# A sparse feed-forward with its pairs taken in three TensorE stages, deeper rings, and targets read from the row itself

## What is computed

```python
topk_idx, topk_weight = _gate(x, gate_w, e_bias)      # 4 of 16 experts per token
g = jnp.einsum('th,eih->eti', x, gate_proj)           # h = 256, i = 128
u = jnp.einsum('th,eih->eti', x, up_proj)
inter = jax.nn.silu(g) * u
expert_out = jnp.einsum('eti,ehi->eth', inter, down_proj)
sel = expert_out[topk_idx, jnp.arange(T)[:, None]]
y = jnp.einsum('tkh,tk->th', sel, topk_weight)
shared_out = jax.nn.silu(hidden_states @ shared_gate_w.T) * (hidden_states @ shared_up_w.T) @ shared_down_w.T
return y + shared_out
```

## Time and profile before

| what | value |
| --- | --- |
| median of 3 runs | 1682.67 us (1679.89 to 1693.12) |
| profiled execution | 1683.4 us |
| its span in the profile | 1681.6 us |
| mean granted TensorE clock | 0.856 of full speed |
| busy over the span | PE 72%, DVE 56%, ACT 47%, GpSimd 32% |

### The profile page before, as it was taken

The page is one execution under the profiler, slowest core; times in us unless marked ns, Lnnn a source line. Parts: engine busy times, 40 slices in busy tenths (PEclk is TensorE's granted clock), DMA queues, the critical chain, the costliest instruction groups (busy, mean ns, idle before and its releaser), DMA issues. The chain is left out here.

```text
span 1681.6 us, 27903 instructions
## 1 busy us (share of the span) xinstructions
PE 1214.9 (72%) x9252; PEld 1108.6 (66%) x9252; DVE 950.1 (56%) x2126; ACT 790.8 (47%) x2137; POOL 529.8 (32%) x590
## 2 busy tenths in 40 slices
PE   3675129995899999999999998667773545478772
PEld 2554128884788888888888887567663535367662
DVE  5886845551766666786677777556641212134664
ACT  4554125451566666666565655346442222245441
POOL 4342263642000010003530356163343342444432
PEclk8766559997999999999999999779886676789886
DMA  3354834545000000002420133276233333344785
GB/s 95 135 160 121 180 120 124 147 116 135 7 8 7 8 20 26 8 1 69 133 64 2 64 127 128 64 224 179 86 123 110 92 106 99 96 145 135 251 281 214
DMA packets 135394, 177.12 MB, mean 105 GB/s; under 512 B 17856, under 2 KB 116320, under 8 KB 135264
## 3 DMA queue, kind: packets, MB, share of 16 engines
q1 hardware_dynamic: 107888, 123.67, 25.3%
q0 software_dynamic: 17792, 43.14, 8.0%
q10 hardware_dynamic: 9584, 8.60, 1.6%
HBM read 107.28 MB, written 68.09 MB: 104 GB/s over the span
## 5 line engine op out<-in xcount | busy, mean ns | idle before, releaser
L1587 ACT ACTIVATE attend_s<-attend_s,attend_less 128x128 f32<-128x128 f32 x512 | 198.3, 391 | 107.8 <-DVE attend_less L1728 104.4
L2199 POOL DMA_INDIRECT answers<-moe_yb,moe_dst x160 | 156.4, 978 | 271.9 <-ACT moe_yb L2264 234.5
L2432 PE MATMUL moe_psX<-const_ident,moe_xg 128*128 128x128 f32 x384 | 71.4, 318 | 133.6 <-DMA moe_xg<-slots 126.7
L2313 DVE TENSOR_TENSOR moe_il<-moe_psI,moe_ih 128x256 fp32r<-128x256 f32 x96 | 40.4, 421 | 216.2 <-ACT moe_ih L2248 209.6
L1198 POOL DMA_INDIRECT slots<-router_row,router_idx x128 | 129.4, 1011 | 101.2 <-DMA router_row<-normed_rows 69.6
L1542 POOL TENSOR_TENSOR router_xn<-rest_acc,router_mv 128x512 f32<-128x512 f32 x12 | 12.5, 1045 | 447.5 <-DVE router_rs L1230 391.3
L2432 PEld LDWEIGHTS moe_psX<-const_ident,moe_xg 128*128 128x128 f32 x384 | 52.7, 163 | 137.1 <-DMA moe_xg<-slots 129.6
L81 PE MATMUL moe_psU<-moe_wh,moe_xl 128*128 (+1 forms) x384 | 131.5, 342 | 0.0
L82 PE MATMUL moe_psU<-moe_wl,moe_xh 128*128 (+1 forms) x384 | 120.2, 313 | 0.0
L83 PE MATMUL moe_psU<-moe_wh,moe_xh 128*128 (+1 forms) x384 | 119.5, 311 | 0.0
L81 PE MATMUL moe_psY<-moe_wh,moe_il 128*128 (+1 forms) x192 | 66.1, 344 | 66.8 <-DVE moe_il L2313 60.0
(11 more groups left out here) (367 smaller groups left out, 4209.4 us busy)
## 6 DMA issues: line engine op xcount, KB each, us to landing
moe_xg<-slots SPq DMA_DIRECT2D x160, 129.0 KB
router_row<-normed_rows SPq DMA_DIRECT2D x64, 256.0 KB
moe_big<-answers SPq DMA_DIRECT2D x16, 1024.0 KB
layer_raw<-in_wi_dram SPq DMA_DIRECT2D x8, 1024.0 KB, 5.0
layer_raw<-in_wo_dram SPq DMA_DIRECT2D x8, 1024.0 KB, 7.0
moe_raw<-in_gex_dram SPq DMA_DIRECT2D x17, 384.0 KB
slots<-moe_big SPq DMA_DIRECT2D x32, 129.0 KB
mix_xin<-in_x_dram SPq DMA_DIRECT2D x8, 512.0 KB, 3.8
```

Of the source, the lines that this page charges most:

```text
L1587: last = nc.scalar.activation(s[:, g, j, :], s[:, g, j, :], ACT.Exp, bias=less[:, g, j:j + 1], accum_out=sm[:, g, j:j + 1])
L2199: nc.gpsimd.indirect_dma_start(out=R.YT[q], out_offset=bass.IndirectOffsetOnAxis(ap=dst[:, j % NX, s:s + 1], axis=0), in_=yb[:, j % NY, s, ...
L2313: v.tensor_tensor(il[:], psI[:, 0:N], ih[:], ALU.subtract).then_inc(i_lo, 1)
L2432: last = nc.tensor.transpose(psX[j % 2][:, k * N + s * P:k * N + (s + 1) * P], xg[:, j % NX, s, k * P:(k + 1) * P], C["ident"][:])
```

## The change

All in `moe`, but for the fillings and the marks of the rows.

- **Three stages.** PE's turn j is now up(j), turn(j+2), turn_inner(j-1), down(j-2). ACT, DVE follow; `ih` and `il` have two places; silu writes into `it`, and `inner` multiplies in place.
- **Rings.** x 6 places, `yb` 5 (routed pairs alone), answers 3 of one batch each, router rows of the last batches 4 halves (in the space of the answers) with a `load_row`, `mark` and `send` of their own.
- **Targets as row bits.** A row's target is written as an integer's bits, so the scatter reads it, and the scaling reads the weight, in the x ring; `targets`, `wd`, `dst` and `d_up` go. A load of the x ring behind a routed pair waits for `scattered` of that pair.
- **Fillings in memory.** `mix` writes the zero rows with their targets once into `fill`, and `padded` copies from there, memory to memory.
- **Order.** 12 shared pairs, 56 + 24 routed, 4 shared. The router's steps come 5 to 6 pairs earlier, sends from pair 22 on. A shared pair's product is added by DVE (`add`) straight from PSUM.
- **Weights.** Two experts per pair; low halves on DVE (even) and GpSimd (odd).
- No drain of GpSimd at the block's end.

```diff
+FIRST, LATE = 12, 4
+KIND = ["shared"] * FIRST + [0] * TILES_OF[0] + [1] * TILES_OF[1] + ["shared"] * LATE
...
-    NX, NY, NR = 4, 3, 2
-    CB = 2
+    NX, NY, NR, NT, NS = 6, 5, 2, 3, 4
...
+        def scattered(eng, r):
+            eng.wait_ge(y_free[r % NY], 32 * (r // NY + 1))
...
             def load(j):
                 b = j % NX
                 if j >= NX:
-                    sp.wait_ge(t_done, j - NX + 1)
+                    if is_shared(j - NX):
+                        sp.wait_ge(t_done, j - NX + 1)
+                    else:
+                        scattered(sp, NTH[j - NX])
...
-                if j - NX >= SHARED_PAIRS:
-                    sp.wait_ge(d_up, j - NX - SHARED_PAIRS + 1)
...
-                sp.dma_start(R.XS[q][bass.ds(row, P), :], pad[:, e, :]).then_inc(pad_in, 16)
+                sp.dma_start(R.XS[q][bass.ds(first, P), :], R.fill[q][e * P:(e + 1) * P, :]).then_inc(pad_in, 16)
+            def load_row(h):
+                b = CHUNKS[LAST][0] + h // 2
+                sp.wait_ge(R.xh_in, 16 * (R.pairs_before(LAST) + h // 4 + 1))
+                if h >= NS:
+                    sp.wait_ge(sent[h % NS], 32 * (h // NS))
+                sp.dma_start(row[:, h % NS, :, 0:D], ...).then_inc(row_in[h % NS], 16)
...
+        answered_from = STARTS_OF[1] + NX + 1
+        for k in range(PART_B[0]):
+            asked_at.setdefault(answered_from + k * 7 // 8, []).append(k)
+            combined_at.setdefault(answered_from + k * 7 // 8 - 3, []).append(k)
...
             def scatter(j):
-                pool.wait_ge(d_up, j - SHARED_PAIRS + 1)
-                pool.wait_ge(y_up, j + 1)
+                r, q = NTH[j], KIND[j]
+                pool.wait_ge(y_up, r + 1)
                 for s in range(2):
-                    ... ap=dst[:, j % NX, s:s + 1] ... in_=yb[:, j % NY, s, :]
+                    ... ap=xg[:, j % NX, s, D + 1:D + 2].bitcast(I32) ... in_=yb[:, r % NY, s, :]
...
-            nc.gpsimd.memset(big[:], 0.0).then_inc(made, 1)
+            for t in range(4):
+                R.send(pool, LAST - 1, t)
+                low(4 * t + 1)
+                low(4 * t + 3)
+            for j in ROUTED:
                 scatter(j)
+                i = j - sends_from
+                if i == 0:
+                    pool.wait_ge(R.idx_up, LAST + 1)
+                if 0 <= i < 2 * HALVES:
+                    if i % 2 == 0:
+                        mark(i // 2)
+                    send(i // 2, i % 2)
...
+            def add(j):
+                dve.wait_ge(y_done, j + 1)
+                a = rows(acc[:, 2 * NTH[j]:2 * NTH[j] + 2, :])
+                v.scalar_tensor_tensor(a, psY[j % 2][:], C["gate"][:, 3:4], a, ALU.mult, ALU.add).then_inc(added, 1)
...
-            for j in range(PAIRS_ALL):
-                if j:
-                    turn_inner(j - 1)
-                up(j, bases)
-                if j:
-                    down(j - 1, former)
+            for j in range(PAIRS_ALL + 2):
+                if j < PAIRS_ALL:
+                    up(j, bases[j])
                 if j + 2 < PAIRS_ALL:
                     turn(j + 2)
+                if 1 <= j <= PAIRS_ALL:
+                    turn_inner(j - 1)
+                if j >= 2:
+                    down(j - 2, bases.pop(j - 2))
```

More of the change, by code:

```diff
@@ L1087, in __init__ @@
         self.YT = [nc.dram_tensor(f"answers{q}", ((PART_B[q] * TOP + 2 * E1) * P, D), F32, kind="Internal").ap() for q in range(2)]
+        self.fill = [nc.dram_tensor(f"fill{q}", (E1 * P, WIDE), F32, kind="Internal").ap() for q in range(2)]
     def stage(self, m):
-        self.spare = m.sb("spare", [P, 2, E1, 2])
+        self.marks = m.sb("marks", [P, 2, 2, E1, 2])
         self.spare_up, self.spare_in = m.sem("spare_up"), m.sem("spare_in")
@@ L1094, in gpsimd @@
         nc = self.nc
[L1095 removed]
+        nc.gpsimd.memset(self.marks[:], 0.0).then_inc(self.spare_up, 1)
         pool.wait_ge(self.spare_up, 1)
         for q in range(2):
[L1098 removed]
+            for kind in range(2):
+                last = nc.gpsimd.iota(self.marks[:, q, kind, :, 1].bitcast(I32), [[P, E1]], base=(PART_B[q] * TOP + E1 * kind) * P, channel_multiplier=1)
         last.then_inc(self.spare_up, 1)
@@ L2134, in answered @@
+                if k >= NT:
+                    store(k - NT)
+                b = k - PART_START[q]
+                sp.dma_start(yt[:, k % NT], R.YT[q][b * P * TOP:(b + 1) * P * TOP, :].rearrange("(p k) d -> p (k d)", k=TOP)).then_inc(yt_in[k % NT], 16)
             def answered(q):
-                last = STARTS_OF[q] + TILES_OF[q] - 1
-                for j in range(last - NY + 1, last + 1):
-                    y_read(sp, j)
+                first = sum(TILES_OF[0:q])
+                for r in range(first + TILES_OF[q] - NY, first + TILES_OF[q]):
+                    scattered(sp, r)
@@ new lines, in _ @@
+            for j in range(NX, PAIRS_ALL):
+                i = j - NX
+                for k in (2 * i + NR, 2 * i + NR + 1):
+                    if k < EXPERTS:
+                        weights(k)
+                if j in (7, 9, 11):
+                    R.load_row(sp, LAST - 1, (j - 5) // 2, 0)
+                    R.load_row(sp, LAST - 1, (j - 5) // 2, 1)
+                if j in (8, 10, 12, 14):
+                    R.store_normed(sp, LAST, (j - 8) // 2)
+                if 7 <= j < FIRST:
+                    for e in range((j - 7) * 4, min(E1, (j - 6) * 4)):
+                        padded(0, e)
+                if j == STARTS_OF[0]:
+                    ready(0)
+                h = j - sends_from - 1
+                if 0 <= h < 2 * HALVES and h % 2 == 0:
+                    load_row(h // 2)
+                e = j - placed_at - NX - 4
+                if 0 <= e < E1:
+                    padded(1, e)
@@ L2167, in _ @@
                 if j == STARTS_OF[1]:
-                    ready(1, LAST + 1)
+                    ready(1)
                 load(j)
-                if j == STARTS_OF[1] + 7:
+                if j == answered_from:
                     answered(0)
-                if j >= STARTS_OF[1] + 7 and asked < COMBINES[0] and (asked < 2 or j >= STARTS_OF[1] + 7 + asked * 8 // 5):
-                    answers(asked)
-                    asked += 1
-            for k in range(asked, COMBINES[0]):
-                answers(k)
@@ L2177, in _ @@
-            answered(1)
-            for k in range(COMBINES[0], sum(COMBINES)):
-                answers(k)
-            store(sum(COMBINES) - 2)
-            store(sum(COMBINES) - 1)
-            sp.wait_ge(stored, 16 * sum(COMBINES))
+                for k in asked_at.get(j, []):
+                    answers(k)
+            for j in range(PAIRS_ALL, answered_from + PART_B[0]):
+                for k in asked_at.get(j, []):
+                    answers(k)
+            answered(1)
+            for k in range(PART_B[0], B):
+                answers(k)
@@ L2184, in _ @@
+            for k in range(B - NT, B):
+                store(k)
+            sp.wait_ge(stored, 16 * B)
         @block.gpsimd
@@ L2419, in _ @@
                     combine(k)
-            i_low(PAIRS_ALL - 1)
-            for k in range(COMBINES[0], sum(COMBINES)):
+            for k in range(PART_B[0] + 4, B):
                 combine(k)
```

331 lines of the change are left out of this document (151 added, 180 removed).

## The result

The changed kernel takes 1700.19 us, the one before 1685.38 us (medians of 20 runs each): ratio 1.0097 [1.0076, 1.0118]. The profiled execution has a span of 1697.9 us against 1681.6, at a granted clock of 0.852 against 0.856. The forecast was 1733 us.

The account below looks back on a forecast made before the run. The send loop was taken as the bound, replaced by a wait for landed scatters: turn(18) at 1198.5, 57 pairs at 6.3 us, 20 at 7.2, then the end, span 1731, time 1733 us (+3.0%); range 1690 to 1780.

Parts of the forecast that it names:

- What bounds the kernel now: Send stretch: a 17.2 us loop per two pairs, SP waiting 164.1 us for sends to land before router-row loads.
- The new loop: Routed loads from j = 18: x-ring places wait for scatters to land; 12.6 us round trip, 6.3 us per pair.
- what would show it: Signs: PE's slot waits everywhere behind pair 17, SP's longest at load, send stretch nearer 6.3, pairs 55 to 74 slower than 4.2.
- The short trip: Rival: nothing queues in the x-ring loop, 10.9 us trip, 5.45 us a pair, about 1660 to 1680 us; chance 0.12.
- the page's rule: Skill page's transfer fit, 2.0 us plus bytes over 436 GB/s: trip some 1.5 us shorter, 5.5 a pair, about 1665 us.
- With the answers: Last 20 loads, from j = 75: answers on SP's queue add 1.8 us to the round trip, 7.2 us per pair.
- The weights: First pairs: two weights per turn take 8 us, four more turns at 4.3, so turn 12 starts at 1175.
- even cycle of 8 us: Weight preparation: two weights through two buffers take 5.7 to 9.4 us per turn, taken as 8, for eight turns.
- The end: After turn(95) at 1701.5: answers asked at 1709.5, last eight batches 21 us, span ending at 1731.
- The sum: Whole span: turn(18) 1198.5, plus 359 for 57 pairs, plus 144 for 20, end 1731; time 1733 us, +3.0%.
- break-even of 5.9 us per pair: Routed pairs: old 80-pair mean of 5.9 us, the point from which the x ring decides faster or slower.
- The ring doesn't bind: Rival: x-ring places come free early enough, pairs run at 4.3 us, 1571 us, 6.6% faster; chance 0.08.

Follow-up runs that it names:

- before3: Kernel before the change, with a third half for the router rows of the last eight batches and nothing else; 1545.26 us, ratio 0.9262.
- dose series: Changed kernel with seven or five x-ring places instead of six, four `yb` places instead of five; seven 1562.97 us, ratio 0.9354; five 2117.46 us.
- copied6: Changed kernel, six places kept, but DVE copies weight and target into rings of eight; load waits for transposes and copy; 1508.81 us, ratio 0.9024.
- twowaits: Changed kernel with a redundant second GpSimd wait before each routed pair's scatters; 1718.99 us, ratio 1.0313; repeated on another chip 1717.78 us, ratio 1.0207.
- copied6_dve: Changed kernel with targets copied by DVE, six places, and all low halves of the weights on DVE, none on GpSimd; 1501.4 us, ratio 0.8996.

## Why the forecast had the direction and not the size

**What bounds the kernel now: right.** The send loop was the bound, and before3 shows its worth, 7%.

**The new loop: right in kind, wrong in size.** The wait for landed scatters took the bound over: the waits on the slots' loads in all stretches, SP's longest wait at load, none for router rows, the send stretch at 6.0 and the pairs behind it at 6.0 to 6.1, slower than 4.2, all as "what would show it" has them. The dose series and copied6 turn it from a reading into a result. The step that failed is the sum of the round trip. Means over pairs 18 to 74 of the trace after:

| term of the trip | forecast, us | measured, us |
| --- | --- | --- |
| end of the product to ScalarE, to the first scatter | 0.1 + 1.6 | 0.1 + 1.21 |
| first to second scatter | 1.27 | 1.27 |
| landing seen, table read, load issued | 2.7 + 0.9 | 3.64 |
| load to transposes | 3.9 | 3.48 |
| transposes to the end of down(j-4) | 2.1 | 2.13 |
| sum | 12.6 | 11.8 |

Two terms carry the error, 0.4 us each. The 1.6 was read from a scatter behind two waits, and the diff showed one of them going; I priced the new instruction by the old one's row (twowaits). With one wait it is 1.11 in 52 of these 57 pairs; five longer ones bring the mean to 1.21. The 3.9 came from a load that stood behind a router row's load of 256 KB on the same queue. All 14 loads of the kernel before that TensorE waited long for have it ahead of them, and take 3.8 us on the mean (3.0 to 4.5; the 3.27 of the earlier trace rows is not the quickest); in the changed kernel those that TensorE waits over 2 us for take 3.3. That the row's load makes the difference is argued, since no run moves it alone. Both errors lie on the same side. Per pair the loop ran at 338.5/57 = 5.94 us for a forecast 6.3: 20.6 us less.

**The short trip, and the page's rule.** The rival's 5.45 us per pair lies 0.49 below the 5.94 found, the forecast 0.36 above it. The Trainium skill (DMA: Bandwidth & Descriptors, section Anatomy of one DMA — SWDGE (gpsimd) path) has its fit for DMAs that GpSimd issues; for the second scatter's 128 KB it would give 2.3 us to landing, an estimate from that page. The trace has 3.64 us with SP's step of some 0.9 in it, so about 2.7, and disagrees by 0.4 us. The forecast had used the fit for SP's load too, which it was not made for: the load took 3.48 us to its use. And put into the forecast's own sum, in place of 2.7 and 3.9, two times 2.3 make the trip 2.0 us shorter, not 1.5.

**With the answers: over-priced.** 1.8 us were added to a trip; 0.7 to 1.4 were found. 20 pairs at 6.31 us and not 7.2: 17.7 us less, of which 7 are the base of 6.3 again. The price had been taken from transfer rates. In the trace after, the time from the second scatter to the load's issue grows from 3.6 us (pairs 54 to 74) to 4.5 (75 to 91), and the time from the load to its use stays at 3.5: the answers delayed the one and not the other.

**The weights: the number right, by luck.** Turn 12 at 1178 for a forecast 1175, turn 18 at 1200.7 for 1198.5. But the even cycle of 8 us is not in the trace: neighbouring transposes stand 2.6 to 8 us apart, but for the three gaps of 15 to 18 us. Eight turns take 60 us for a forecast 64, the next four take 28 for 17, and pairs 12 to 17 then go at 2.9 us each for 4.3, so that the errors cancel. I had also put pair 12 of the kernel before at 1160, and its trace has it at 1153. Which step sets the first pairs remains open, weights or router: the low halves' engine moved pair 12 by 5 us, the fill copies by 1, and no run moved the router's turns.

**The end.** 32.4 us behind the transposes of pair 95 for a forecast 29.5.

**The sum.** +2.2 - 20.6 - 17.7 + 2.9 = -33.2 us: 1731 becomes 1697.9, the measured span. Against the kernel before: pair 18 comes 19.1 us later (1200.7 for 1181.6), pairs 18 to 95 take 464.8 us for 459.4, and the end takes 32.4 for 40.6. These make 16.3 us, the difference of the spans. The forecast had +44 us in those 77 pairs, and the loop gave 5 of them; what makes the kernel slower is the start with its weights and router, 19 us. So the direction was right in part by luck. The removed loop and the new one cost the same within 1.2% over those 77 pairs, which is why a change of this size moved the time by 1%. My break-even of 5.9 us per pair was sound; the forecast lay 0.4 above it and the kernel lay on it.

**The ring doesn't bind: unlikely as said, and mis-sized too.** With the ring off the path the kernel takes 1509 us, where I had 1571. I had let TensorE go at 4.3 us per pair, from the third line of the earlier trace rows, read as TensorE at its own pace. It was not: PE was busy 56.5 of its 72 us, and its transposes there mostly come 2.8, 3.7 and 5.0 us apart in turn. Freed, it went at 2.9 to 3.9.

## What to carry to other kernels

When a copy out of a ring is removed so that a later reader takes its data from the ring itself, count the new life of a place up to the landing of the last reader, divide that trip by the places left over from the engines' own stages, and compare it with the pace of each stretch and not of the whole: here saving two small DVE copies per pair cost more than 10% of the time. When a row of before prices a step of after, look at what stands in front of it there, waits and transfers alike, and strike out what the diff strikes out. A change that fixes one bound and builds another looks like no change at all; run its parts one by one before it is dropped.

## What the hardware did that I had not expected

- A second semaphore wait in front of an indirect DMA on GpSimd, for a count reached long before, costs 0.48 us: from ScalarE's start to the scatter it is 1.11 us with one wait (75 of 80 pairs of the changed kernel, never less) and 1.59 to 1.60 with two (69 of 80 in twowaits, never less). In the other pairs it is longer.
- The faster the loop, the faster TensorE, in these runs. In the stretch of pairs 54 to 75 the granted clock was 0.79 with six places and waits, and 1.00 with the targets copied. A product of 256 columns took 0.41 us behind a wait and 0.28 in the steady stretch of copied6_dve. A stall costs itself and the slower work behind it.
- The trip stayed near 12 us because two things in it ran against each other. From the second scatter to the use of the new load it took 3.23 + 2.88 = 6.1 us with five places (DMA share 0.21), 7.1 with six (0.40), 4.09 + 3.88 = 8.0 with seven (0.57). TensorE's part, from the transposes to the scaling that begins the next trip, fell from 2.9 to 2.2 and 1.8 us, as the granted clock of the stretch rose from 0.65 to 0.79 and 0.93.
- The DMA engines showed a busy share of 1.02, as this profile counts it, and 368 GB/s beside TensorE at 0.95 of its clock, in the last stretch of copied6_dve; the earlier trace rows had 0.82 and 266 at most.
